# Attention with routed experts on one core: the bf16 splits of keys and queries move from GpSimd to VectorE

## What is computed

```python
# q, k, v: projections, split into 16 heads of 16
q = heads(layernorm(x) @ Wq + bq); k = heads(ctx @ Wk + bk); v = heads(ctx @ Wv + bv)
logits = einsum('bhqd,bhkd->bhqk', q, k) / sqrt(16) + mask * -1e9
x = x + merge(softmax(logits) @ v) @ Wo + bo
# experts: scores = softmax(layernorm(x) @ w_gate), top 2, at most 1024 tokens for an expert
x = x + sum_over_top2(score * (silu(a) * g) @ c_proj[e]),   [a, g] = layernorm(x) @ c_fc[e]
```

## Time and profile before

| | us |
|---|---|
| median of 3 runs | 466.71 (462.95 to 474.04) |
| profiled execution | 464.91 |
| its span, first to last instruction | 463.2 |
| busy: TensorE (matmul) | 375.9 (81% of the span) |
| busy: VectorE | 261.6 (56%) |
| busy: ScalarE | 212.5 (46%) |
| busy: GpSimd | 178.1 (38%) |

### The profile page before, as it was taken

The page is one execution under the profiler, slowest core; times in us unless marked ns, Lnnn a source line. Parts: engine busy times, 40 slices in busy tenths (PEclk is TensorE's granted clock), DMA queues, the critical chain, the costliest instruction groups (busy, mean ns, idle before and its releaser), DMA issues.

```text
span 463.2 us, 9267 instructions
## 1 busy us (share of the span) xinstructions
PE 375.9 (81%) x2712; PEld 295.9 (64%) x2713; DVE 261.6 (56%) x688; ACT 212.5 (46%) x339; POOL 178.1 (38%) x181
## 2 busy tenths in 40 slices
PE   0647888886996978969587769987999999999990
PEld 0533556554573645735354449975999999999980
DVE  3726565698696996968968854632233333333330
ACT  1440365566373573735336337542354444454440
POOL 5552061343362562725230512622243443344332
PEclk9965889899897998979889877998999999999997
DMA  7399378692937829168040552443433234323340
GB/s 229 121 196 181 66 151 185 173 216 76 222 109 158 207 91 202 58 145 162 22 153 4 167 176 80 115 83 72 66 60 59 44 58 68 60 47 60 65 57 4
DMA packets 65431, 51.77 MB, mean 112 GB/s; under 512 B 11880, under 2 KB 62328, under 8 KB 65400
## 3 DMA queue, kind: packets, MB, share of 16 engines
q1 hardware_dynamic: 57224, 42.36, 39.6%
q0 software_dynamic: 7008, 8.43, 10.7%
q10 hardware_dynamic: 1168, 0.59, 0.5%
HBM read 32.89 MB, written 19.06 MB: 112 GB/s over the span
## 4 chain that ended last, share of the span: by engine, by line
PE 48%; DVE 26%; DMA 9%; issue 6%; SPq 3%; ACT 3%; POOL 1%; ACTq 1%; POOLq 0%; DVEq 0%
PE bank L930 18%; PE bank L941 8%; DVE NEG L1046 8%; PE bank L820 5%; PE bank L786 4%; PE bank L885 3%; PE bank L856 3%; DVE bn L1003 2%; PE bank L869 2%; PE bank L793 2%; DMA out<-CTt,GG 2%; DVE AVT L1065 2%; DMA wf<-qparts_d 2%; PE bank L910 1%; DVE AVN L1068 1%
## 5 line engine op out<-in xcount | busy, mean ns | idle before, releaser
L930 PEld LDWEIGHTS bank<-XN,KS 128*128 128x128 f32 x912 | 110.8, 197 | 5.5 <-ACT KS L719 2.4
L930 PE MATMUL bank<-XN,KS 128*128 128x128 f32 x912 | 111.7, 280 | 2.2 <-ACT KS L719 1.3
L680 ACT ACTIVATE PR<-bank 128x512 f32<-128x512 f32 x128 | 73.0, 593 | 80.0 <-PE bank L869 68.5
L1046 DVE TENSOR_REDUCE NEG<-bank 128x2 f32<-128x512 f32 x128 | 83.5, 683 | 42.5 <-PE bank L856 41.8
L580 POOL DMA_INDIRECT out<-CTt,GG x38 | 58.9, 1550 | 109.5 <-DMA out<-CTt,GG 80.0
L719 ACT ACTIVATE KS<-wf 128x1536 f32 x40 | 59.4, 1488 | 51.5 <-PE bank L930 45.1
L856 PE MATMUL bank<-KS,wf 99*128 99x256 bf16 x256 | 52.1, 288 | 22.7 <-DVE NEG L1046 15.1
L941 PE MATMUL bank<-wp,QF 128*128 x228 | 56.8, 386 | 2.6 <-DVE CTt L1276 2.5
L1262 DVE COPY XN<-bank 128x256 f32<-128x256 f32 x39 | 16.5, 424 | 71.7 <-PE bank L910 71.5
L869 PE MATMUL bank<-wf,KS 102*128 102x256 bf16 x256 | 49.5, 277 | 6.3 <-ACT PR L680 5.6
L856 PEld LDWEIGHTS bank<-KS,wf 99*128 99x128 bf16 x256 | 20.3, 102 | 47.6 <-DVE NEG L1046 30.9
(11 more groups left out here) (165 smaller groups left out, 466.7 us busy)
## 6 DMA issues: line engine op xcount, KB each, us to landing
wf<-in_L_ffn_c_fc SPq DMA_DIRECT2D x8, 768.0 KB, 5.7
XG<-slots SPq DMA_DIRECT2D x40, 128.0 KB
kparts_d<-KP SPq DMA_DIRECT2D x8, 384.0 KB, 2.5
qparts_d<-QP SPq DMA_DIRECT2D x8, 384.0 KB, 2.6
KS<-kparts_d SPq DMA_DIRECT2D x8, 384.0 KB
KS<-kparts_d SPq DMA_DIRECT2D x24, 128.0 KB
wf<-qparts_d SPq DMA_DIRECT2D x8, 384.0 KB
wf<-qparts_d SPq DMA_DIRECT2D x24, 128.0 KB
```

Source lines behind the costliest of these rows:

```text
L680: act.activation(PR[:, s % NPROB, :], STB[s % 2][:], ACT.Exp).then_inc(exp_done, 1)
L930: ins = pe.matmul(bank[2 + 2 * u + g][:, c * P:(c + 1) * P], UP[u][:, (k * 2 + g) * FF + c * P:(k * 2 + g) * FF + (c + 1) * P], XTG[:, u, ...
L1046: dve.tensor_reduce(NEG[:, n % 2, t, 2 * hp:2 * hp + 2], MXB[m % 2][:].rearrange("p (i s) -> p i s", i=2), AX.X, ALU.max, negate=True).the ...
```

## The change

For the batches 2 to 7 the four subtractions of the split go to VectorE's stream, each in a unit of its own: rest of the keys in unit 1, rest of the queries in unit 2, last part of the keys in unit 4, last part of the queries in unit 5 of stage n - 2, each behind the maximum of its unit and ahead of the statistics, the slots and the normalized product. ScalarE's second parts move from units 1 and 2 to units 3 and 4 for these batches; for the batches 0 and 1 everything stays. GpSimd has no split any more.

```diff
@@ AT
-    "second K": 5, "second Q": 6,
+    "second K": 7, "second Q": 8, "second K of the first": 5, "second Q of the first": 6,
+    "rest K": 5, "rest Q": 6, "last K": 8, "last Q": 9,
@@ gpsimd
                 for n in projected(it):
-                    if n >= 2:
-                        split(pool, n)
-                    else:
+                    if n < 2:
                         ones_rows(n + 1)
@@ scalar
-                    for n in projected_at(it, u, AT["second Q"]):
+                    for n in projected_at(it, u, AT["second Q of the first" if it == -2 else "second Q"]):
                         second_part(n, QP, QREST, qrest_ready, qd_out, qp1_ready)
                     if 0 <= it < B:
                         exponentials(it, u)
-                    for n in projected_at(it, u, AT["second K"]):
+                    for n in projected_at(it, u, AT["second K of the first" if it == -2 else "second K"]):
                         second_part(n, KP, KREST, krest_ready, kd_out, kp1_ready)
@@ vector
                     if u == AT["split 1"] and 0 <= it < B:
                         split_max(it, 1)
+                    for n in projected_at(it, u, AT["last K"]):
+                        if n >= 2:
+                            last_of_keys(dve, n)
+                    for n in projected_at(it, u, AT["last Q"]):
+                        if n >= 2:
+                            last_of_queries(dve, n)
+                    for n in projected_at(it, u, AT["rest K"]):
+                        if n >= 2:
+                            rest_of_keys(dve, n)
+                    for n in projected_at(it, u, AT["rest Q"]):
+                        if n >= 2:
+                            rest_of_queries(dve, n)
                     if u == AT["slots"] and 0 <= it - 2:
                         route_slots(it - 2)
```

More of the change, by code:

```diff
@@ L310, in last_part, with rest_of_keys, rest_of_queries, last_of_keys @@
             eng.tensor_tensor(parts[:, :, 2, :], by_chunk(rest[:]), parts[:, :, 1, :], ALU.subtract).then_inc(done, 1)
+        def rest_of_keys(eng, n):
+            first_rest(eng, n, KF, KP, KREST, kp0_ready, krest_ready, kp_ready)
+        def rest_of_queries(eng, n):
+            first_rest(eng, n, QF, QP, QREST, qp0_ready, qrest_ready, qp_ready)
+        def last_of_keys(eng, n):
+            last_part(eng, n, KP, KREST, kp1_ready, kp_ready)
+        def last_of_queries(eng, n):
+            last_part(eng, n, QP, QREST, qp1_ready, qp_ready)
         def split(eng, n):
[L313 to L316, removed]
+            rest_of_keys(eng, n)
+            rest_of_queries(eng, n)
+            last_of_keys(eng, n)
+            last_of_queries(eng, n)
         block = es.enter_context(nc.Block())
```

## The result

The changed kernel takes 472.37 us (median of 20 runs, 465.92 to 1065.66; one run far off the others does not move the median), the kernel before 469.73 beside it (20 runs). The medians differ by 2.6 us. The ratio, which compares the fast runs of the two alone, is 1.0077 with a 95% interval of 1.0049 to 1.0105, which is 3.6 us of 469.7. That is within 2%, and the time is inside the range I gave, but it is a loss, not the "no change" I forecast (0.2 us on 466.7). Two more measurements of the same kernel gave 1.0056 and 1.0072. The profiled execution has 471.79 us and a span of 470.0, 6.8 more than before.

A forecast was written before the change was run, and what follows sets the result against it. VectorE's instructions in front of ON were taken to bound stages 1 to 5. Terms of -2.0 (stages 2 to 5), +1.4 (stage 1) and +0.8 (stage 0) gave +0.2 us, so 466.9 us; range 460 to 473.5.

The forecast's parts named there:

- Prices of the moved instructions: 24 subtractions at 0.69 us each on VectorE, 16.6 us more; lost and slotf, freed of stalls, at 0.17 and 0.16.
- Stages 2 to 5 in front of ON: VectorE's two rest subtractions per stage ahead of ON, less freed stalls: -2.0 us in sum.
- Stage 1: Two rest subtractions in front of ON, with no slots there to be freed: +1.4 us.
- Stage 0: Four subtractions, no ON, VectorE waiting for the bias product: +0.8 us, bounds 0 and 2.8.
- Last parts hidden: Units 4 and 5 of stages 1 to 5: 0.69 us each in VectorE's idle 2.98 and 1.57 us, costing nothing.
- rival B: Key and query loads too late for the next stage's first row-maximum matmul: slower, about 479 us; chance 0.06.
- What becomes late next: SyncE queue: query parts complete 8.0 us later, loads shift 7 us but stay hidden, weights delay nobody; 0 in the sum.
- rival C: Little row loads of the maxima come late at stage ends: 2 to 6 us, 469 to 473; chance 0.13.
- The clock: TensorE's clock falling in other places was named as a sign that the prediction is wrong; no size given.
- rival A: Freed stalls win and TensorE's output projection reaches full clock in four stages: faster, about 457 us; chance 0.09.
- V: Theory from the experiments: the loss comes from VectorE's own work and from TensorE's clock.
- R: Theory from the experiments: late loads hold up the maxima's row loads; changed kernel with both moves at 0.996 to 1.002.

The follow-up runs named there:

- both moves: Scatter at the head of GpSimd's part of a stage, bias add right behind it: kernel before 0.9868 and 0.9946, changed kernel 1.0021 and 1.0136, late stores 1.0014.
- scatter first: Changed kernel with GpSimd's scatter of stages 2 to 5 at the head of its part of the stage: 468.08 us, ratio 1.0033.
- late stores: Kernel before, splits on GpSimd, with SyncE holding the key and query stores until the maxima of units 4 and 5: 472.48 us, ratio 1.0103.
- the three combinations of the second group: Changed kernel with the parts one unit sooner and scatter first; the same and weights first; scatter first and weights first only: 1.0176, 1.0147, 1.0119.
- weights first: Changed kernel with expert weights and next context of stages 1 to 5 issued ahead of the key and query stores: 469.92 us, ratio 1.0025.
- the parts one unit sooner: Changed kernel with ScalarE's second parts and VectorE's last parts each one unit earlier: 467.17 us, ratio 1.0067.

## Why the prediction was right or wrong

- **Prices of the moved instructions: right.** I foresaw 0.69 us, and 0.68 to 0.69 were measured. `lost` and `slotf` fell to 0.17 and 0.16, as read from the earlier trace rows.
- **Stages 2 to 5 in front of ON: right.** -2.0 us foreseen, -2.3 measured (table, second column). The wait of the output projection is 14.2 us in five (12.7 before), none over 3.0; the 1.5 more are all in stage 1 (0.60 to 2.10).
- **Stage 1: +1.4 foreseen, +1.9 measured.** The rest goes with the row loads between stages 0 and 1, 5.53 us before and this after, on the chain that ended last:

```profile
72.91 6.31 DMA wf<-NMT
```

- **Stage 0: +0.8 foreseen, +0.2 measured.** The rests lie ahead of maxima for which VectorE waits.
- **Last parts hidden: right.** The idle stretches shrank from 2.98 and 1.57 to 2.38 and 1.20 us, by 0.6 and 0.4 where I gave 0.7 each.
- **Loads in time (rival B): right.** No instruction after waits for the parts behind stage 0.
- **"What becomes late next": this is the step that failed.** Its times held. The query store of stage 3 came at 152.82, with the stage 3.1 us late, so at 149.7 against the 150 that I gave; the traffic ended at 170.4 - 3.1 = 167 where I had about 166. What I made of it did not: the weights "wait for nobody in this phase". I asked who waits for those bytes, and not what else would run while they did. The scatter and the row loads stand beside them, in other queues. I priced the row loads alone (rival C), and at zero. In stages 2 to 5 the stage ends cost 3.8 us, with TensorE's signals up to 2.9 us late.
- **Rival C was nearest, by its number more than by its mechanism.** It gave 469 to 473 for row loads that come late. In the changed kernel the matmuls wait for them 1.4 us (0.6 before) from 50 to 224 us, in one wait at the start of stage 1, and the stage ends of 7.6 us come mostly from TensorE's late signals. Only with the scatter and the bias add away do the row loads reach C's upper end of 6 us: 5.8 and 6.3 us by the matmuls, 7.6 and 7.7 by the weight loads. I had set the Trainium skill's rule of DMA engines that take turns between queues packet by packet (DMA: Bandwidth & Descriptors, Queues, rings and completion order) against it. The traces do not agree: in the changed kernel with both moves, from the last issue (161.76) to the first packet of that queue (165.31) over 1000 packets of the SyncE queue move and none of this one. Nor does the 5.53 us of the earlier trace rows speak for a late completion count, as I read it, since the packets themselves start late: there, in the kernel before, the first issue is at 71.64 and the first packet at 76.53. What holds them back is not shown.
- **The clock: left out of the sum.** I took it up only as a gain (rival A), and named it among the signs that I am wrong. That sign came: behind `ON` it cost 3.2 us in stages 1 to 5, and in front of `ON` 1.7 us in stage 6. Which part of that follows from the idle time at the stage ends is not shown: with the scatter first in the changed kernel, `ON` to unit 6 stayed as long (7.0, 6.6, 6.7, 5.4 us in stages 2 to 5) although the stage ends were short. With late stores alone it was 6.3, 6.2, 6.0 and 5.5, against 5.5, 6.6, 5.3 and 6.2 in the kernel before. It moves with where the low stretches fall. The changed kernel has three profiles, all with a long stretch here, but the kernel before has one, and that does not settle it. So V's part in this column stays open.

So the sum over the instructions was right to about 1 us. That the time fell into my range all the same is in part luck: I had widened it for the row loads, stage 0 and the spread of the runs, and not for late signals or a lower clock. The step that failed had costed at nothing seven to eight microseconds of lateness in a queue. What the experiments settle is that this lateness by itself makes a loss as large as the one measured, and that TensorE's signals are late only when it meets the scatter. With both moves made, the times and the waits for the row loads rise together, which argues for the row loads but leaves 3.8 us between late stores and the changed kernel that R did not foresee. What stays open besides is how GpSimd's scatter beside a full SyncE queue delays TensorE's signals, how much of the lower clock belongs to the moved subtractions, and why the three combinations of the second group were slower than their traces explain.

## What to carry to other kernels

When a change makes a transfer late, do not stop at who waits for its bytes: lay the whole queue, shifted, over the other queues, and name each small transfer and each indirect one that it now meets. Here 16 us more work on VectorE cost nothing in front of `ON` (-0.5 us in sum), and stores 7 to 8 us later, with no work moved, cost as much as the whole change. An instruction on GpSimd that reads two large inputs is best put where VectorE waits for another engine; moving this bias add and the scatter gave 0.987 and 0.995 of the time before, and moving 24 subtractions gave a loss.

## What the runs showed of the hardware that I had not expected

- **TensorE's signals can be late for two engines at once.** They reach VectorE 2.1 to 2.9 us late and ScalarE 3.0 us (stage 3 of the changed kernel), while TensorE runs on, and the lateness is over some 1.1 us after the last instruction of the scatter. It was there in every kernel with stores as late as the changed one's and the scatter at the stage's end (three profiles of the changed kernel, late stores, weights first; 5.3 to 5.4 us in two waits for "remote" or 8.2 to 8.3 in three). It was in none with the scatter at the stage's head, and neither in the kernel before nor with the parts one unit sooner.
- **Small loads on one queue can stand still beside another full queue.** The first packet of the row loads moves 1.3 us behind the first issue when the SyncE queue is quiet, and 5.2 to 5.6 us at the ends of stages 1 to 5 in the three profiles of the changed kernel.
- **A GpSimd instruction of 128x512 also holds VectorE instructions on 128x256 float32.** 1.53 in place of 0.43 us, begun within 0.01 us of the bias add, over when it is. The Trainium skill (GPSIMD Engine Reference, Key points) has contention between the two for instructions with two SBUF inputs, and this row agrees.
- **The DMA engines are wholly busy at 91 to 153 GB/s and at 345 to 441,** first with what I take for the loads of the parts, then with the weights. The share of busy time says nothing of how much is moved.
